# Low one-hot rows kept in DRAM between two sums, and blocks applied eight at a time in the second

## What is computed

```python
# second stage: attention over edges
a = e_exp / denom[dst]
out = jax.ops.segment_sum(a[:, None] * nfeat[src], dst, num_segments=n)

# third stage: two graph convolutions with plain sums
agg = jax.ops.segment_sum(h[src], dst, num_segments=n)      # twice, weights all 1

# fourth stage: given edge weights
messages = x[src] * edge_weights[:, None]
out = jax.ops.segment_sum(messages, tgt, num_segments=x.shape[0])
```

## Time and profile before

| what | value |
|---|---|
| time, median of 3 runs | 5457.6 us (5450.8 to 5461.4) |
| profiled execution, first to last instruction (span) | 4809.8 us |
| median less span: what lies around it | 647.8 us |
| PE busy / DVE busy / ACT busy | 80% / 74% / 44% of the span |
| first sum | about 1653 to 2960 us of the span |
| blocks, twice, and their products | about 3000 to 3740 |
| second sum | 3771 to about 4780 |
| instructions on PE and PEld | 108027 each |
| DMA | 405.03 MB, mean 84 GB/s |

### The profile page before, as it was taken

How to read it: one execution, slowest core, us unless ns; L and a number is a source line. 1 busy time by engine, 2 the same in 40 slices (tenths; PEclk the granted TensorE clock), 3 DMA queues, 4 the chain that set the end, 5 groups by cost and what they waited for, 6 DMA issues and landing times.

```text
span 4809.8 us, 236947 instructions
## 1 busy us (share of the span) xinstructions
PE 3862.8 (80%) x108027; PEld 3145.8 (65%) x108027; DVE 3543.1 (74%) x4279; ACT 2094.6 (44%) x2437; POOL 911.8 (19%) x810
## 2 busy tenths in 40 slices
PE   5541966949458588888989886999999699999997
PEld 4531865949448466666666664998899566666665
DVE  5985675786767877777777776555655899999996
ACT  5200102010020277777777774664665355444543
POOL 0565747644224330000000000000000000000000
PEclk9975785968759699999999997998999799999998
DMA  6742342724306211111111111553554000000000
GB/s 161 251 141 35 102 140 74 201 75 130 112 22 178 65 53 54 55 52 56 54 52 53 54 54 59 177 180 123 181 180 147 6 11 11 10 10 11 10 11 17
DMA packets 240114, 405.03 MB, mean 84 GB/s; under 512 B 110098, under 2 KB 167700, under 8 KB 239364
## 3 DMA queue, kind: packets, MB, share of 16 engines
q1 hardware_dynamic: 213768, 383.12, 25.8%
q0 software_dynamic: 25472, 10.79, 1.2%
q10 hardware_dynamic: 184, 0.08, 0.0%
HBM read 287.89 MB, written 110.03 MB: 83 GB/s over the span
## 4 chain that ended last, share of the span: by engine, by line
PE 70%; DVE 11%; issue 7%; POOL 3%; ACT 3%; DMA 2%; DVEq 0%; SPq 0%; ACTq 0%
PE psum L1120 20%; PE psum L1093 15%; PE psum L1160 13%; PE psum L921 10%; PE psum L1081 4%; POOL heads_d L611 2%; PE psum L889 2%; POOL gath L619 1%; DVE space L1645 1%; PE psum L863 1%; PE psum L877 1%; PE psum L1169 1%; ACT space L770 1%; DVE space L1430 1%; PE psum L1002 1%
## 5 line engine op out<-in xcount | busy, mean ns | idle before, releaser
L775 ACT COPY space<-psum 128x784 f32<-128x784 f32 x1184 | 966.1, 816 | 615.6 <-PE psum L1093 613.4
L1093 PE MATMUL psum<-space 64*128 64x49 bf16 x56832 | 991.6, 185 | 166.0 <-issue 137.0
L1093 PEld LDWEIGHTS psum<-space 64*128 64x128 bf16 x56832 | 855.5, 95 | 377.1 <-issue 269.4
L1120 PE MATMUL psum<-space,X 128*64 128x256 f32 x7252 | 1040.0, 395 | 14.3 <-issue 11.3
L1645 DVE TENSOR_TENSOR space<-space 128x2352 bf16<-128x2352 bf16 x592 | 814.6, 1376 | 0.0
L921 PE MATMUL psum<-table,space 128*128 128x56 bf16 x24300 | 682.8, 189 | 119.7 <-DVE space L1300 75.7
L921 PEld LDWEIGHTS psum<-table,space 128*128 128x128 fp8e4 x24300 | 669.0, 97 | 133.4 <-issue 120.1
L1639 DVE TENSOR_TENSOR space<-space,V 128x2048 bf16<-128x2048 bf16 x592 | 721.2, 1218 | 0.0
L1160 PE MATMUL psum<-space 128*128 128x192 bf16 x7252 | 627.7, 247 | 10.7 <-ACT space L808 10.7
L1297 DVE TENSOR_REDUCE space<-psum 128x1512 f32 (+1 forms) x300 | 518.4, 1730 | 147.2 <-PE psum L921 142.3
L1160 PEld LDWEIGHTS psum<-space 128*128 128x128 bf16 x7252 | 594.3, 98 | 36.4 <-issue 35.7
(11 more groups left out here) (283 smaller groups left out, 2763.9 us busy)
## 6 DMA issues: line engine op xcount, KB each, us to landing
space<-adj_d SPq DMA_DIRECT2D x148, 784.0 KB, 4.3
space<-onehots SPq DMA_DIRECT2D x240, 432.0 KB
adj_d<-space SPq DMA_DIRECT2D x222, 192.0 KB, 2.0
onehots<-space SPq DMA_DIRECT2D x60, 432.0 KB, 3.4
space<-digit_rows SPq DMA_DIRECT2D x60, 378.0 KB
adj_d<-space SPq DMA_DIRECT2D x74, 208.0 KB, 2.0
space<-cw_d SPq DMA_DIRECT2D x37, 160.0 KB, 2.3
cw_d<-space SPq DMA_DIRECT2D x4, 1184.0 KB, 13.2
```

Of the source, the lines that this page charges most:

```text
L775: nc.scalar.copy(A[:, h, :, b * P:(b + 1) * P].rearrange("p a (w s) -> p w a s", w=2)[:, :, :, c:c + UC], psum[:, 2 + 2 * (k % 2):4 + 2 * ...
L1093: mm = nc.tensor.matmul(psum[:, 2 + 2 * (k % 2) + w, c * NB:(c + 1) * NB], ohlo[lo:hi, ring, col // 2, :, col % 2], ohw[lo:hi, ring, r, co ...
L1120: mm = nc.tensor.matmul(pb[6][half:half + F, 0:2 * P], X[:, a, :], A[:, 1 - h, a, :], start=(a < 2), stop=(a >= NB - 2))
```

## The change

In the first sum the low one-hot rows of each step are stored to a new DRAM tensor `lo_hot` (296 steps of 128x2048 bf16, 512 KB each) as soon as they are made. VectorE waits for the store of a buffer (`oh_saved`) before it writes it again. In the second sum VectorE no longer makes `ohlo`; SP loads it from `lo_hot` into a ring of four buffers, the two old ones and two more in the place of `adj`, and PE waits for the load (`oh_loaded`). SP loads step t+4 when PE has finished step t. SP's order in the first sum is written anew so that the stores of `adj` and of the low rows alternate. Besides, in the second sum the block products stand eight sub-blocks behind every second unit (`PARTS_OF = [4, 8]`); in the first sum they stay at four behind each.

```diff
-PART = 4
-EVERY = PART // 4
+PARTS_OF = [4, 8]
+RING = 4
...
+        lo_hot = dram("lo_hot", (NDB * HS, P, HC * P), BF16)
...
+        lo_ring = [[ohlo[:, 0], ohlo[:, 1]], [ohlo[:, 0], ohlo[:, 1], lo_more[:, 0], lo_more[:, 1]]]
...
+            def store_lo(i, h, t):
+
+                sp.wait_ge(codes_ready, i * (2 * HS) + (h * HS + t + 1))
+                sp.sem_inc(sp_ok, 1)
+                sp.dma_start(lo_hot[row_of(i, h * HS + t, 2 * HS)].rearrange("a p x -> (a p) x"),
+                             lo_ring[0][t % 2].rearrange("p s a e -> p (s a e)")).then_inc(oh_saved[t % 2], 16)
+
+            def load_lo(i, at, r):
+                sp.dma_start(lo_ring[1][r].rearrange("p s a e -> p (s a e)"),
+                             lo_hot[row_of(i, at, 2 * HS)].rearrange("a p x -> (a p) x")).then_inc(oh_loaded[r], 16)
...
+            def counted_pair(i, h, more=True, first=False):
+
+                before = (i, 0) if h else (i - 1, 1)
+                for t in range(HS):
+                    store_lo(i, h, t)
+                    if t < 2 and not first:
+                        for q in (2 * t, 2 * t + 1):
+                            store_counts(*before, 1, q)
+                    if t in (4, 5):
+                        for q in (2 * t - 8, 2 * t - 7):
+                            store_counts(i, h, 0, q)
+                if more:
+                    next_codes(0, i, h)
...
+            def loaded_pair(i, h, more=True, last=False):
+
+                for t in range(HS - RING if last else HS):
+                    sp.wait_ge(wgt_psum, i * (4 * GU) + (NDB * 2 * GU + 2 * (h * HS + t + 1)))
                     sp.sem_inc(sp_ok, 1)
...
+                    load_lo(i, h * HS + t + RING, t % RING)
+                    if more and t == HS - 2:
+                        next_codes(1, i, h)
...
+                low = lo_ring[n][k // 2 % len(lo_ring[n])]
...
+                    if n:
+                        pe.wait_ge(oh_loaded[k // 2 % RING], LOADED + 16 * ((hot - NDB * HS - 1) // RING + 1))
...
-                        done = (k + 1) // EVERY * PART
-                        for a in range(done - PART, min(done, NB)) if (k + 1) % EVERY == 0 else range(done, NB) if k == MIXED - 1 else ():
+                        each = PARTS_OF[n]
+                        done = (k + 1) // (each // 4) * each
+                        for a in range(done - each, min(done, NB)) if (k + 1) % (each // 4) == 0 else range(done, NB) if k == MIXED - 1 else ():
...
-                nc.vector.tensor_tensor(ohlo[:, ring, :, :, :], pairs_of(cw[:, h, t * HC:(t + 1) * HC], P), table(P), ALU.is_equal).then_inc(codes_ready, 1)
+                if n == 0:
+                    if not (isinstance(i, int) and i + h == 0 and t < 2):
+                        dve.wait_ge(oh_saved[ring], i * (16 * HS) + (SAVED + 16 * ((h * HS + t) // 2)))
+                    nc.vector.tensor_tensor(lo_ring[0][ring], pairs_of(cw[:, h, t * HC:(t + 1) * HC], P), table(P), ALU.is_equal).then_inc(codes_ready, 1)
```

More of the change, by code:

```diff
@@ L506, in codes_in @@
                     sp.dma_start(cw[:, h, 0:codes_of[n]], cw_d[n, h, :, 0:codes_of[n]]).then_inc(cw_loaded[h], 16)
-            def store_counts(i, h, b, last=False):
-                for q, (lo, hi) in enumerate(STORES):
-                    sp.wait_ge(adj_made, i * (4 * GU) + ((2 * h + b + 1) * GU + (0 if last else q)))
-                    sp.sem_inc(sp_ok, 1)
-                    at = slice(4 * i + 2 * h + b, 4 * i + 2 * h + b + 1) if isinstance(i, int) else bass.ds(i * 4 + (2 * h + b), 1)
-                    sp.dma_start(adj_d[at, :, lo * P:hi * P].rearrange("b p x -> (b p) x"),
-                                 adj[:, b, lo:hi, :].rearrange("p a s -> p (a s)")).then_inc(adj_stored[b], 16)
@@ L517, in pair @@
-            def pair(n, i, h, more=True):
-                if n == 0:
-                    store_counts(i, h, 0)
-                if more:
-                    sp.wait_ge(hot_ready, i * (2 * HS) + (n * NDB * HS + (h + 1) * HS))
-                    sp.sem_inc(sp_ok, 1)
-                    at = slice(2 * i + h + 2, 2 * i + h + 3) if isinstance(i, int) else bass.ds(i * 2 + (h + 2), 1)
-                    sp.dma_start(cw[:, h, 0:codes_of[n]], cw_d[n, at, :, 0:codes_of[n]].rearrange("d p x -> (d p) x")).then_inc(cw_loaded[h], 16)
-                if n == 0:
-                    store_counts(i, h, 1, isinstance(i, int) and 2 * i + h == NDB - 1)
@@ L530, in pairs, with row_of, store_counts @@
-            def pairs(n):
+            def row_of(i, at, each):
+                return slice(i * each + at, i * each + at + 1) if isinstance(i, int) else bass.ds(i * each + at, 1)
+            def store_counts(i, h, b, q, last=False):
+                lo, hi = STORES[q]
+                sp.wait_ge(adj_made, i * (4 * GU) + ((2 * h + b + 1) * GU + (0 if last else q)))
+                sp.sem_inc(sp_ok, 1)
+                sp.dma_start(adj_d[row_of(i, 2 * h + b, 4), :, lo * P:hi * P].rearrange("b p x -> (b p) x"),
+                             adj[:, b, lo:hi, :].rearrange("p a s -> p (a s)")).then_inc(adj_stored[b], 16)
@@ new lines, in counted_pairs @@
+            def counted_pairs():
+                counted_pair(0, 0, first=True)
+                counted_pair(0, 1)
+                with sp.Fori(1, NDB // 2 - 1) as i:
+                    for h in range(2):
+                        counted_pair(i, h)
+                counted_pair(NDB // 2 - 1, 0)
+                counted_pair(NDB // 2 - 1, 1, more=False)
+                counted_pair(NDB // 2, 0, more=False)
+                for q in range(len(STORES)):
+                    store_counts(NDB // 2, 0, 1, q, last=True)
@@ L535, in pairs @@
-                pair(n, NDB // 2 - 1, 0)
-                pair(n, NDB // 2 - 1, 1, more=False)
-                pair(n, NDB // 2, 0, more=False)
+                        loaded_pair(i, h)
+                loaded_pair(NDB // 2 - 1, 0)
+                loaded_pair(NDB // 2 - 1, 1, more=False)
+                loaded_pair(NDB // 2, 0, more=False, last=True)
             codes_in(0)
@@ L542, in _ @@
             sp.dma_start(sums_d.rearrange("(p t) a -> p (t a)", t=TF), zF).then_inc(sums_stored, 16)
-            pairs(0)
+            counted_pairs()
             def apply_loads(n):
@@ L569, in _ @@
             apply_loads(1)
-            pairs(1)
+            sp.wait_ge(mm_read, 2 * NMG)
+            for r in range(RING):
+                sp.wait_ge(oh_saved[r % 2], SAVED + 16 * (NDB * HS // 2))
+                load_lo(0, r, r)
+            loaded_pairs()
             sp.wait_ge(x_ready, 2 * LAYERS + 6)
@@ L1080, in products_of_unit @@
                             lo, hi = KC * w, KC * w + KC
-                            mm = nc.tensor.matmul(psum[:, w, c * NB:(c + 1) * NB], ohlo[lo:hi, ring, col // 2, :, col % 2],
+                            mm = nc.tensor.matmul(psum[:, w, c * NB:(c + 1) * NB], low[lo:hi, col // 2, :, col % 2],
                                                   ohhi[lo:hi, ring, col // 2, :, col % 2], start=True, stop=True)
@@ L1092, in products_of_unit @@
                             lo, hi = KC * w, KC * w + KC
-                            mm = nc.tensor.matmul(psum[:, 2 + 2 * (k % 2) + w, c * NB:(c + 1) * NB], ohlo[lo:hi, ring, col // 2, :, col % 2],
+                            mm = nc.tensor.matmul(psum[:, 2 + 2 * (k % 2) + w, c * NB:(c + 1) * NB], low[lo:hi, col // 2, :, col % 2],
                                                   ohw[lo:hi, ring, r, col // 2, :, col % 2], start=(r == 0), stop=(r == 2))
```

12 lines of the change are left out of this document (10 added, 2 removed).

## The result

The kernel after takes **5580.4 us** in the median of five runs (5553.1 to 5586.6), beside 5457.6 us before (5448.6 to 5461.4, five runs): **1.0215 times as long, 95% interval 1.0191 to 1.0238**. By that ratio it is 117 us more; the medians are 123 us apart. 5584 us were forecast, 126 more.

What follows compares the result with a forecast made beforehand. The prediction took PE and its instruction supply to bound the first sum and PE's own work the second; +59 us in the second and +67 in the first made +126 on 5457.6, so 5584 us, range 5400 to 5705.

Steps and rivals of the forecast that it cites:

- (e): Second sum: the loads lengthen a block's round trip to 4.15 us, range 3.94 to 4.40, giving 28.6 us a pair.
- rival C: Both sums: traffic costs all that a busy pick stage shows, 4.40 us a block; 5725 us, within the forecast's 0.66.
- full trip of 3.94 us: PE's instructions: time from one block's start to the next when PE is through with it sooner, in quiet stretches.
- (a): Second sum: VectorE loses 9.7 us of work a pair, but only its 0.54 us wait comes back to PE.
- (b): Second sum: sub-blocks in eights make six turns fewer in a pair and save 0.8 us.
- (c): Second sum: PE's own work falls to 25.4 us a pair, but 6.9 packets at 3.94 us need 27.1 us.
- The step of 0.21 us a block: First sum: with the stores each of 8.9 blocks a pair comes 0.21 us later, 1.85 us a pair.
- A: Both sums: instruction supply stays hidden, a second-sum pair saves 1.35 us, the first sum stays; 5403 us, chance 0.17.
- B: Both sums: traffic leaves the round trip at 3.94 us, the first sum stays; about 5463 us, chance 0.12.
- D: Both sums: transfers come late, loads over 10 us or stores over 8 us; 5750 us or more, chance 0.05.

Runs made afterwards that it cites:

- both pairs of runs: Fewer matmul pieces: two of three in the second sum, 23.79 us a pair with loads, 23.90 without; one of three in the first, 27.91 with stores, 28.81 without.
- second profile of before: The kernel before, unchanged, profiled once more: 5468.6 us with a span of 5466.4 us.

## Why the prediction was right

**The bound.** "What is late next when DVE is out of the way is the instruction supply" was the step on which all hung. It held: all gaps of the second sum stand at blocks of 256 instructions, behind a packet that has just come, and none is for DVE; half the loss is in each sum; with fewer instructions it is gone (in both pairs of runs); with no traffic the pair stays a microsecond above PE's own work.

**That the sum came out to 3 us is in part luck.** The unknown of (e), 4.15 us for a block under traffic, charged to each of 6.9 blocks, holds two errors that cancel. A block that is really late took 4.43 us after in the second sum, about what rival C took from the pick (4.40). But not every block is late: there are 75 gaps for 231 packets. The run without loads shows the same on its own, 26.39 us a pair where a full trip of 3.94 us for each block gives 27.1. That the packets came 4.11 us apart in the mean, and 4.20 in the first sum, confirms the time of the pairs and not the trip of a block.

**The second sum**, forecast +59 us, 28.6 us a pair: measured +54 and 28.29. (a) and (b), the 0.54 us of DVE's wait and the 0.8 us of the turns, can be read from the run without loads together with its waits: 26.39 less 1.0 us of "issue" (33.0 us in 34 pairs) is 25.4, the sum of (c). This too is a net figure: PE's busy time fell by 1.2 us a pair (868.8 us in 33.6 pairs to 840.8 in 34.1), and its waits for ScalarE rose by 0.4. The whole can be made up from waits. Per pair there are 2.2 us more of "issue" (76 against 3 in 33.6 pairs), 0.4 more of waits for ScalarE and some 0.5 for the clock (0.98), less 0.5 and 0.8: 1.8, of which 1.5 are measured. Two terms were wrong in it: the clock I had not in my sum, and "the 0.33 us wait for ScalarE, which a late block hides" was not hidden but doubled, to 0.67 us a pair (13.6 and 8.8 us in 33.6 pairs).

**The first sum**, forecast +67 us, 1.85 us a pair: measured +52 and 1.36. The direction and the place were right, the term was too large by a third. By waits: 4.3 us a pair for "issue" against 3.5, all of the rise in gaps at blocks, and the clock's 0.94 to 0.92. "PE there runs at about the speed at which its instructions come" holds less than I thought: the first profile had no short stops, and in the executions that were timed they are a third of the gaps' time before, with nothing of the supply in them. The step of 0.21 us a block was too large too, as far as the late ones show it: they went from 4.20 to 4.32 us in the mean, with a wide spread, and more blocks were late (103 gaps instead of 86). The other 9 of the 52 us fall in the first three pairs, which take 46 us each against 43 before. (A slip without effect: the second stretch of rows 2 is 857.5 us long, not 857.3.)

**The rivals.** A, the supply hidden, would need 25.4 us a pair; not even without loads is it reached. The rule of the Trainium skill (Runtime: NRT & Kernel Launch, "Instruction fetch mechanics") that crossing from one block to the next is "mostly hidden" holds for the kernel before in its second sum, with 3.3 us of such waits in 900 us. It does not hold for its first sum (61 us of gaps at blocks in 1000), nor for either sum of the kernel after (86 us in 1000 and 70 in 950). B fell with the run without loads: 1.9 us hang on the loads. D was not there: loads land within 5.7 us and stores within 4.9. At what traffic it would come was not tried, since twice the loads came late by their order on SP.

**What was wrong** is the base: "The 647.8 us between span and median lie outside of what the change touches." 604 of them lie ahead of the first sum, but inside the span, and 52 lie in the first sum itself, which the change does touch; the first profile was of a quicker execution. It did no harm to the sum since I added differences to the median, but the same execution also gave the 34.8 us a pair of the first sum, without the short stops.

## What to carry to other kernels

Where an engine's program is written out, count its instructions and look for gaps that stand 256 of them apart. In this kernel the blocks that PE had to wait for came 3.9 us (quiet) to 4.4 us (with loads) apart in the mean, so a stretch that needs less for 256 instructions is in danger of being held up by the supply, whatever the engines' busy shares say. Work taken from another engine then gains little (here 0.4 us a pair of VectorE's 9.7), and transfers beside it can cost more than that, so price new traffic by what it does to the blocks that are already late before asking whether it is hidden. The mean distance of the packets is no measure of the supply: take the blocks that begin and end with a gap. See where a gap stands before blaming the supply for it: 64 of 150 in the first sum of before were something else. And compare a profile's span with the timed runs before adding to it: a gap of more than a few microseconds can mean that the profile is of another kind of execution.

## What the runs showed of the hardware

In every execution profiled after the first, the picks ahead of the first sum have stretches in which PE does one to six matmuls and stops, mostly for 0.4 to 1.2 us, over and over, with no semaphore behind it. From the timeline of PE in the second profile of before:

```profile
613.36 0.28 PE L921 MATMUL psum<-table,space 128*128 128x56 bf16 x4 [1.01 <-issue]
614.80 0.29 PE L921 MATMUL psum<-table,space 128*128 128x56 bf16 x5 [1.16 <-issue]
```

These are not blocks of 256 instructions. In the first profile of the same kernel there are 11 such stops ahead of the first sum, in the second 305, and the first sum begins 604 us later. The same pattern stands in the first three pairs of the first sum and once in most pairs behind them, before and after. The stops keep near the transfers that GpSimd issues: 265 of the 305 and 62 of the 64 in the first sum's steady stretch lie within 1 us of one. But the first profile has the same transfers and hardly a stop, so they are not enough by themselves. What brings the stops on was not tried.

The granted clock fell behind gaps of PE and not with traffic: 0.93 in the second sum with two pieces and no loads, 0.95 with loads, 1.00 with three pieces and no loads. Nor does it go by how long PE stands still in all: that is 58 of 899 us in the last of these (clock 1.00) and 44 of 815 in the first (0.93).
